# Causal mask of the first layer's row maxima: added by VectorE inside the maximum instead of by two TensorE products per head

## The reference

```python
Q = _rope(heads(Wq)); K = _rope(heads(Wk)); V = heads(Wv)
causal = jnp.tril(jnp.ones((S, S), dtype=bool))
def attend(q, k):
    s = (einsum(q, k) + LAMBDA * einsum(q * q, k * k)) * inv_sqrt_d
    s = jnp.where(causal, s, -1e9)
    a = jax.nn.softmax(s, axis=-1)
    return einsum(a, V)
...
x = x + _L0_attn_ref(_layernorm(x), ...)
x = x + _L0_ffn_ref(_layernorm(x), ...)      # 512 hidden, relu
x = x + _L1_attn_ref(_layernorm(x), ...)     # not causal
x = x + _L1_ffn_ref(_layernorm(x), ...)      # 384 hidden, silu gate, int32 weights
```

## Time and profile before

| | us |
|---|---|
| time, median of 3 runs (361.4 to 362.06) | 362.04 |
| time of the profiled execution | 363.09 |
| its span, first to last instruction | 361.3 |
| PE / DVE / ACT / POOL busy in the span | 311.9 / 254.3 / 221.5 / 155.7 |

### The profile page before, as it was taken

One profiled execution on the slowest core, in us unless ns is written; L12 is line 12 of the kernel. 1 busy time (PEld: TensorE's weight loads), 2 busy tenths in 40 slices (PEclk: granted clock), 3 DMA queues, 4 the chain that ended last, 5 costly groups with the idle time before them and its releaser, 6 DMA issues.

```text
span 361.3 us, 8503 instructions
## 1 busy us (share of the span) xinstructions
PE 311.9 (86%) x3088; PEld 227.1 (63%) x3088; DVE 254.3 (70%) x642; ACT 221.5 (61%) x493; POOL 155.7 (43%) x367
## 2 busy tenths in 40 slices
PE   1771688897998999899999899999999999998754
PEld 1551566675776777686767576666666675765443
DVE  5784678677575676667676857777988989883423
ACT  5355256767566576557566666867776777677401
POOL 6262536757474765647484815230220303022020
PEclk9987869899999999999999999999999999999968
DMA  7677212324012122313100010101111110100000
GB/s 203 218 165 179 66 59 83 93 58 121 19 36 71 47 75 62 97 48 91 31 2 29 2 40 15 53 23 53 35 39 37 37 38 26 39 1 17 15 2 29
DMA packets 23033, 21.27 MB, mean 59 GB/s; under 512 B 2896, under 2 KB 20048, under 8 KB 22992
## 3 DMA queue, kind: packets, MB, share of 16 engines
q1 hardware_dynamic: 22992, 20.73, 20.7%
HBM read 13.24 MB, written 7.34 MB: 57 GB/s over the span
## 4 chain that ended last, share of the span: by engine, by line
PE 64%; POOL 10%; ACT 9%; DVE 8%; issue 6%; DMA 1%; POOLq 0%; ACTq 0%; SPq 0%; DVEq 0%
PE bank L869 15%; PE bank L843 6%; PE bank L901 4%; PE bank L910 4%; PE bank L944 4%; ACT PB L500 3%; PE bank L820 3%; PE bank L847 3%; PE bank L821 3%; POOL PB L393 3%; PE bank L936 3%; PE bank L780 3%; PE bank L918 2%; PE bank L817 2%; PE bank L878 2%
## 5 line engine op out<-in xcount | busy, mean ns | idle before, releaser
L650 DVE TENSOR_REDUCE NM<-bank 128x3 f32<-128x384 f32 (+1 forms) x256 | 148.2, 615 | 48.2 <-PE bank L817 33.2
L500 ACT ACTIVATE PB<-bank 128x384 f32<-128x384 f32 (+1 forms) x256 | 131.9, 547 | 38.6 <-PE bank L845 21.7
L843 PE MATMUL bank<-QS,KS 128*128 128x256 f16 x256 | 70.6, 277 | 5.8 <-ACT PB L500 4.9
L869 PE MATMUL bank<-PB,VP 128*32 128x256 f32 (+1 forms) x1024 | 61.7, 358 | 5.9 <-POOL PB L393 5.8
L869 PEld LDWEIGHTS bank<-PB,VP 128*32 128x32 f32 x1024 | 26.7, 109 | 29.3 <-POOL PB L393 9.7
L393 POOL TENSOR_SCALAR_AFFINE_SELECT PB<-PB 128x512 f32<-128x512 f32 x64 | 41.9, 655 | 0.0
L418 POOL TENSOR_TENSOR xs<-xs,Y 128x256 f32<-128x256 f32 x8 | 5.8, 726 | 77.7 <-DVE Y L664 77.7
L843 PEld LDWEIGHTS bank<-QS,KS 128*128 128x128 f16 x256 | 24.9, 97 | 18.4 <-ACT PB L500 15.5
L817 PE MATMUL bank<-KS,QS 96*128 96x256 f16 x128 | 36.2, 283 | 0.0
L820 PE MATMUL bank<-KS,QS 96*128 96x256 f16 x128 | 35.2, 275 | 0.8 <-DVE NM L650 0.8
L821 PE MATMUL bank<-KS,QS 96*128 96x256 f16 x128 | 34.6, 271 | 0.0
(11 more groups left out here) (93 smaller groups left out, 616.3 us busy)
## 6 DMA issues: line engine op xcount, KB each, us to landing
scr<-PR SPq DMA_DIRECT2D x16, 256.0 KB, 2.8
QS<-scr SPq DMA_DIRECT2D x16, 128.0 KB, 2.6
QS<-scr SPq DMA_DIRECT2D x32, 64.0 KB, 2.8
KS<-scr SPq DMA_DIRECT2D x32, 64.0 KB, 2.8
KS<-scr SPq DMA_DIRECT2D x16, 128.0 KB, 3.0
scr<-PR SPq DMA_DIRECT2D x16, 128.0 KB, 1.9
out_x<-xs SPq DMA_DIRECT2D x8, 128.0 KB, 1.9
W<-in_w SPq DMA_DIRECT2D x1, 576.0 KB, 6.1
```

The source lines that it names most:

```text
L500: act.activation(PB[:, s % RING, 0:n], TB_[s % 2][:, 0:n], ACT.Exp).then_inc(s_e, 1)
L650: dve.tensor_reduce(NM[i % 2][:, s, 0:n], SB_[g % 3][:, 0:w].rearrange("q (n k) -> q n k", n=n), AX.X, ALU.max, negate=True).then_inc(s_mx, 1)
L843: pe.matmul(o[:, 0:S], k[:, 0:P], q[:, :], start=True, stop=True)
L869: ins = pe.matmul(o, v, pr, start=(g % 2 == 0 and kt == 0), stop=True, skip_group_check=True)
```

## The change

`scores` loses the two mask products in layer 0: two products per head remain, into the same columns. `maximum` in layer 0 becomes two fused operations of VectorE, each of which adds the mask (float32, in SBUF) to a part of the score bank, scales by -1, and takes the minimum over all columns, with 3e38 as the start. The first has 128 columns, with the triangle; the second 256, with a plane of zeros and the triangle. Each writes its full result, which nobody reads, to JUNK in bfloat16, and its minimum to a column of NM. The merged NMB and its operation and semaphore go; `max_rows` takes both columns from NM and waits for the maxima in both layers alike. The masks are no longer narrowed to bfloat16, and their load has two planes instead of three. DVE now waits for that load ahead of the first maximum, and PE no longer waits for the narrowed masks.

```diff
-        MSF = sb("MSF", [P, 3, P])
-        MSK = sb("MSK", [P, 3, P], BF16)
+        MSF = sb("MSF", [P, 2, P])
+        JUNK = sb("JUNK", [P, 3, 3, P], BF16)
...
-            dve.wait_ge(s_msf, 16)
-            dve.tensor_copy(MSK[:, :, :], MSF[:, :, :]).then_inc(s_msk, 1)
...
+            dve.wait_ge(s_msf, 16)
+
             def maximum(i, s):
                 g = H * i + s
-                n, w = (3, 384) if ORDER[i][0] == 0 else (2, 512)
+                m, o = NM[i % 2], SB_[g % 3]
                 dve.wait_ge(s_s, g + 1)
-                dve.tensor_reduce(NM[i % 2][:, s, 0:n], SB_[g % 3][:, 0:w].rearrange("q (n k) -> q n k", n=n),
-                                  AX.X, ALU.max, negate=True).then_inc(s_mx, 1)
-                if ORDER[i][0] == 0 and s % HC == HC - 1:
-
-                    dve.wait_ge(s_mx, g + 1)
-                    cs = slice(s + 1 - HC, s + 1)
-                    dve.tensor_tensor(NMB[i % 2][:, cs], NM[i % 2][:, cs, 1], NM[i % 2][:, cs, 2], ALU.min).then_inc(s_mb, 1)
+                if ORDER[i][0] == 0:
+
+                    dve.tensor_tensor_reduce(JUNK[:, g % 3, 0], o[:, 0:P], MSF[:, 1], -1.0, 3e38, ALU.add, ALU.min,
+                                             accum_out=m[:, s, 0:1])
+                    dve.tensor_tensor_reduce(JUNK[:, g % 3, 1:3], o[:, P:3 * P].rearrange("q (n k) -> q n k", n=2), MSF[:, :], -1.0,
+                                             3e38, ALU.add, ALU.min, accum_out=m[:, s, 1:2]).then_inc(s_mx, 1)
+                else:
+                    dve.tensor_reduce(m[:, s, 0:2], o[:, :].rearrange("q (n k) -> q n k", n=2), AX.X, ALU.max,
+                                      negate=True).then_inc(s_mx, 1)
...
                 if L == 0:
-                    pe.matmul(o[:, 0:P], MSK[:, 0], MSK[:, 1], start=True, stop=True)
-                    pe.matmul(o[:, 0:P], q[:, 0:P], k[:, 0:P], start=False, stop=True, skip_group_check=True)
-                    pe.matmul(o[:, 2 * P:3 * P], MSK[:, 0], MSK[:, 1], start=True, stop=True, skip_group_check=True)
-                    ins = pe.matmul(o[:, P:3 * P], q[:, P:2 * P], k[:, :], start=False, stop=True,
-                                    skip_group_check=True)
+                    pe.matmul(o[:, 0:P], q[:, 0:P], k[:, 0:P], start=True, stop=True)
+                    ins = pe.matmul(o[:, P:3 * P], q[:, P:2 * P], k[:, :], start=True, stop=True)
...
-                if L == 0:
-                    pe.wait_ge(s_mb, 2 * b + c + 1)
-                else:
-                    pe.wait_ge(s_mx, H * i + HC * (c + 1))
+                pe.wait_ge(s_mx, H * i + HC * (c + 1))
...
-    masks = np.stack([np.eye(P, dtype=np.float32), upper, upper.T], 1)
+    masks = np.stack([np.zeros((P, P), np.float32), upper], 1)
```

More of the change, by code:

```diff
@@ L145, in program @@
         PB = sb("PB", [P, RING, 2 * S])
-        NM = [sb(f"NM{p}", [P, H, 3]) for p in range(2)]
-        NMB = [sb(f"NMB{p}", [P, H]) for p in range(2)]
+        NM = [sb(f"NM{p}", [P, H, 2]) for p in range(2)]
         MT = [[sb(f"MT{p}{c}", [HC, S], F16) for c in range(2)] for p in range(2)]
@@ L178, in program @@
         s_v1 = sem("v_spread_ones")
-        s_msk = sem("masks_narrowed")
         s_prep = sem("small_prepared")
@@ L195, in program @@
         s_s, s_mx = sem("scores"), sem("maxima")
-        s_mb = sem("maxima_merged")
         s_mi = [sem(f"maxima_in_{c}") for c in range(2)]
@@ L799, in _ @@
                 project_v(b)
-            pe.wait_ge(s_msk, 1)
             for k in range(3):
@@ L832, in max_rows @@
                 pe.transpose(m[0:HC, 0:P], NM[i % 2][:, cs, 0], IDF[:, :])
-                pe.transpose(m[0:HC, P:2 * P], NMB[i % 2][:, cs] if L == 0 else NM[i % 2][:, cs, 1],
-                             IDF[:, :]).then_inc(*fills(f"mr{c}", i))
+                pe.transpose(m[0:HC, P:2 * P], NM[i % 2][:, cs, 1], IDF[:, :]).then_inc(*fills(f"mr{c}", i))
             def shifted(i, s):
```

## The result

The kernel after takes 359.74 us (median of 20 runs) against 362.32 us before on the same occasions: ratio 0.9933, 95% interval 0.9916 to 0.9951. That is 2.4 us faster by the ratio and 2.6 by the two medians. Timed again later, beside other kernels, the ratio was 0.9919 (0.9887 to 0.9952). The profiled execution's span fell from 361.3 to 358.0 us.

A forecast was written before the change was run, and what follows sets the result against it. Steady phases of layer 0 were taken as bound by DVE's queue, closely followed by POOL's, in slots 8 to 14. Steady phases -0.65 and start -1.0 us gave 362.04 - 1.65 = 360.4 us, range 357.4 to 364.6.

The forecast's parts named there:

- PE does not bound a phase of layer 0: In layer 0's phases other queues set PE's next start at three places, so the full 14.7 us is not gained.
- C: Rival: PE's queue bounds everything, so the full 14.7 us is gained, 347.3 us; chance 0.03.
- Heads 2, 3, 6, 7: Only these heads of a steady phase are PE's own on the path; they lose 4 x 0.115 = 0.46 us.
- M: Time of a head's masked maximum on DVE: 0.65 us taken, 0.457 today; prediction wrong if outside 0.57 to 0.70.
- A: Rival: the column of minima on DVE is free (M = 0.53), 4.35 us faster, 357.7 us; chance 0.20.
- 141.32 + 4M: Slots 8 to 14: start of head 14's third product with V, 143.92 at M = 0.65, against 144.05 now.
- B: Rival: DVE becomes the bound, with M = 0.81 and PE waiting before head 14; +2.25 us, 364.3 us; chance 0.27.
- From there to the next phase unchanged: After slot 14's third product with V, PE's long products, ACT and POOL set the path; nothing gained or lost.
- rival D: Rival: same M, but another shift, such as DVE's L692 lengthening the cut in all phases, +1.65 us, 362.0 us; chance 0.08.
- The start: Before 90 us: mask products gone give -0.84 and -0.45, DVE's longer maxima +0.3; together -1.0 us.
- The merge, the masks' narrowing and the load: Merging operation and narrowing on DVE removed, mask load a third shorter: nothing on the path; merge 0.6 us a phase at most.
- the signs to look for: Profile after: wait ahead of second feed-forward half about 0.35 us, head 14's scores over 0.19, last product with V about 1.4.

The follow-up runs named there:

- run 3: Kernel before without the mask products in slots 2, 3, 6 and 7 alone, maxima there leaving the mask out: 359.79 us, ratio 0.9936.
- run 4: Kernel before without the mask products in the twelve slots other than 2, 3, 6 and 7: 361.82 us, ratio 0.9998.
- run 1: Kernel before without its two mask products per head; reduction and merge stay, maxima leave the mask out: 358.24 us, ratio 0.9915.
- run 6: Kernel after with a third fused operation per head on DVE, repeating the 128-column one: 368.67 us, ratio 1.0194 to the kernel before.
- run 7: Kernel after with DVE's low halves of layer 1's q and k ahead of the bias addition: 358.34 us, ratio 0.9913 to the kernel before.
- run 8: Kernel after with ACT's cast of layer 1's q and k moved behind exponential 15: 352.17 us, ratio 0.9745 to the kernel before.
- run 9: Kernel before, with nothing of the change, and ACT's cast of layer 1's q and k behind exponential 15: 357.39 us, ratio 0.9852.
- run 2: Kernel before with the fused maxima and without the merge; mask products stay, so the mask is added twice: 364.22 us, ratio 1.0073.
- run 5: Kernel after with two more one-column writes ahead of each pair of fused maxima: 360.12 us, ratio 0.9945 to the kernel before.

## Why the prediction came out right

The time was forecast as 1.65 us less, 360.4, in a range of 357.4 to 364.6; 2.4 to 2.6 us less were measured. By its steps:

- **PE does not bound a phase of layer 0: right.** Runs 3 and 4 show it directly. C, with its 14.7 us, is refuted by run 1.
- **Heads 2, 3, 6, 7 are worth 0.46 us: right** (0.46 in run 3). That other heads are worth nothing was too strict: slots 8 to 10 give 0.11 in b and those up to slot 14 give 0.06 in c, shown by run 4.
- **M: mis-sized.** I took 0.65 us, with 0.06 for each column of minima, and 0.555 is what the trace has. There are two instructions for one, as the prediction said, but the second costs about 0.01 us of the queue (0.555 less the 0.53 of the two main operations, halved). M lies between A and my forecast and outside the 0.57 to 0.70 that I had set for the latter; by this sign, which the prediction had named itself, the forecast's M failed, and A's 0.53 was nearer.
- **141.32 + 4M: right.** The four maxima on the path took 1.63 us (137.44 to 139.07) and 0.52, 2.15 us. That gives 143.47, 0.58 us earlier, which is what the phase has. Run 6 confirms the factor of four (0.85 us for 0.21 a head), from close to rival A's M to close to B's. One reading in the sum was off without consequence: `project_o` is done at 140.9, not 140.8.
- **"From there to the next phase unchanged": failed.** I had the collision of low halves and cut as rival D, at 1.65 us and a chance of 0.08, in a sum with the forecast. It happened in full: 1.4 us by stretch d. Run 7 changes nothing but DVE's order and takes most of it away in its trace, 0.4 us a phase, so it is these two operations. Run 8 agrees, but its move shortens ACT's chain as well.
- **The start:** 1.0 forecast. The two traces give 1.45 (90.42 to 88.97 at the last product of the phase before the steady ones), but a second trace of the kernel after has 89.75 there, which makes it 0.67, and the execution traced before was 0.8 us slower than that kernel's median. What the times leave beside the 1.5 us of the five phases is 0.9 to 1.1. So the size fits, while its parts were not tested, and two of them were off: DVE has 10 maxima between 52 and 60.4 us, not 12, with 0.16 us of idle at 58.16; and PE's granted clock moved, which the sum left out and D had named:

```profile
30.00:50.00 20.00, 11.60 (x68) 9.17 (x69) 11.85 (x31) 7.77 (x14) 8.40 (x20) 0.71 0.43 101
60.00:70.00 10.00, 8.13 (x98) 5.98 (x88) 6.97 (x17) 7.69 (x17) 6.81 (x17) 0.83 0.31 89
```

```profile
30.00:50.00 20.00, 11.51 (x46) 8.25 (x47) 12.04 (x66) 7.71 (x13) 8.18 (x20) 0.59 0.37 97
60.00:70.00 10.00, 6.60 (x79) 4.14 (x79) 7.88 (x50) 7.67 (x17) 6.88 (x16) 1.00 0.32 95
```

The first pair of windows is before, the second after. Between 30 and 50 us the granted clock was 0.71 before and 0.59 after, between 60 and 70 us 0.83 and 1.00; the second trace of the kernel after has the same 0.59 and 1.00. What each is worth stays open.

So the number came out near by luck in part: two errors offset each other. With the measured M the steady phases would have been put at -2.55 instead of -0.65 and the start at about -1.3, nearly -3.9 us in all. The collision, put at nothing in the forecast, took 1.4 of it, and what is left is close to what was measured. That runs 8 and 9 give 3.8 to 3.9 without the collision is no proof of this sum: their parts are 2.2 and 1.9. The merge, the masks' narrowing and the load had been costed at nothing on the path, and no run tests them singly. Since runs 1 and 2 both collide, neither the merge's absence nor the missing products is needed for it; how much of the roughly 0.2 us by which DVE comes earlier in the kernel after is due to the merge stays open.

Of the signs to look for, the wait ahead of the second feed-forward half (0.35 us) and of head 14's scores (0.34) came as said; the one ahead of the last product stayed at 1.02 instead of 1.4 us. The time that heads 15, 0 and 1 lose now passes earlier: PE comes 0.26 us behind head 0 to L916 instead of 0.06, and head 1 waits 0.22 us for an exponential.

## What to carry to other kernels

Split a phase at the points where a queue waits, and ask of every removed instruction in which stretch it lies: here a quarter of the removed products carried 0.46 of the 0.63 us that a to c gained in runs 3 and 4. Then ask what the shift does to pairs of operations on DVE and POOL that exclude each other: with 0.03 us between them the order decides over 0.5 us a phase, and moving one cast behind an exponential, which ended the collision and shortened ACT's chain, was worth more (7 us) than the whole change. A pair of traces is one sample of each kernel: two traces of the same kernel differed by 0.8 us in their start. A dose of extra work is only a dose if the trace shows that it took the time.

## What the runs showed that was not expected

- Reading the accumulator: 83 ns in its row, about 0.01 us in the distance to the next operation (0.21 and 0.345 us, against the 0.20 and 0.33 of operations of the same widths in the earlier trace rows).
- Two one-column writes ahead of a longer operation of DVE cost 0.035 us together (run 5), though such a write alone had 0.06 to the next start.
- A subtraction on DVE with both inputs in SBUF (0.68 us) held up even a one-column addition on POOL from 0.19 to 0.70 us when it began 0.03 us earlier. The fused operations, one input in PSUM and one in SBUF, did not: of the 64 cuts of the kernel after, 62 took 0.63 to 0.64 us, and the two of 1.09 are collisions with the low halves. Both agree with the Trainium skill (SBUF — State Buffer, "Who interferes with whom").
- PE's clock at 0.63 over 8.26 us of run 6, behind 4.79 us in which PE was half busy, cost 2.7 us; behind a similar stretch of the kernel after it did not fall.
